# A decoder layer on one Trainium2 core: a second buffer for transposed probabilities, maxima of two heads in one instruction, and another order of the cross-attention loop

## The chip, the core and the metric

The kernel runs on one core of a Trainium2 chip. The metric is the device time of one execution in microseconds (us), the median of several runs. The engines are PE (TensorE, matmuls and transposes), DVE (VectorE), ACT (ScalarE), POOL (GpSimd) and SP (SyncE, which issues most DMAs).

## What is computed

A pre-norm decoder layer over 8 sequences of 100 tokens and width 512, all in float32. The part that matters here is the cross-attention, with 16 heads of size 32 and 345 context tokens:

```python
x = x + self_attention(layernorm(x))            # 16 query heads, 4 key/value heads
q = ln(layernorm(x) @ Wq + bq)                  # per head of 32
k, v = ln(y_main @ Wk + bk), y_main @ Wv + bv   # 345 context tokens, width 256
s = einsum('bhqd,bhkd->bhqk', q, k) * SCALE
p = softmax(s, axis=-1)
ctx = einsum('bhqk,bhkd->bhqd', p, v)           # + the same over 16 further tokens (dca)
x = x + ctx @ Wo + bo
x = x + shared_expert(h) + sum of 4 of 60 routed experts, h = layernorm(x)
```

## The kernel before

The eight sequences are done in four pairs by a hardware loop (`Fori(0, PAIRS)`). Within a pair, PE first does self-attention and the key/value projections of the context, while POOL normalises the heads of the keys and of the queries one after the other (`head_norm` in the POOL program, L654 to L678). Then comes the cross-attention loop, which the change edits. After the last pair follow the router, the shared expert and the routed experts.

The cross-attention loop has ten steps, t = 0 to 9. A "four" is a group of four heads of one sequence; a pair of sequences has eight fours. In step t, PE

- computes the scores of four t (`four_scores`, L913): four products of 32 contraction rows each, into PSUM banks 0 to 3, once ACT has emptied these banks;
- multiplies the values of four t-2 (`four_values`, L935), 12 products, and ahead of four 0 and of four 4 a product of zeros that opens the accumulation in bank 6 or 7 (L930);
- transposes the probabilities of four t-1 (`four_transposes`, L922) in three parts c = 0, 1, 2 of 115 context tokens, alternating between banks 4 and 5;
- runs a hook: in step 0 the query projection of the second sequence (L787), in step 3 the transpose of its normalised queries (L805), in step 4 its scores against the 16 further tokens (L883), in step 5 two more transposes (L891, L947) and the end of the context sum (L900), in step 6 the output projection of the first sequence (L787), in step 8 another transpose (L891).

DVE finds each head's maximum over 345 scores (`four_max`, L1666), ACT computes the exponentials from it (`four_exp`, L1276), and DVE copies the transposed parts from PSUM to SBUF (`four_T`, L1670; part 1 of the last four is copied by ACT, L1325). There is one buffer `xpT` for the three parts. Between these, DVE does pieces of the layer norms of the next pair's inputs (`few(n)` takes n pieces). In step 7 it adds the output projection to the residual (L1637) and starts the last layer norm of the pair. ACT's `q_T(1)` (L1234) copies the second sequence's queries, which the scores of step 4 need.

Each engine runs its own program in the order in which it is written, and semaphores join them. A bank has a "full" and a "free" signal, counted over all fills of the bank in the order that `attention_fills` lists, so the list has to agree with PE's order.

After step 9 the pair ends with a transpose (L781), the router gate and the output projection of the second sequence (together 16 instructions of L787), a residual and a layer norm on DVE, and stores; POOL starts the next pair when the store of x2 has landed (L631).

## Time and profile before

| | us |
|---|---|
| median of 3 runs | 1371.33 |
| lowest and highest | 1367.48, 1371.35 |
| the profiled execution | 1366.12 |
| span in its trace | 1364.3 |

The profile is of one execution. "Granted clock" is the clock that the chip gave TensorE: 1.00 stands for 2.4 GHz and 0.50 for 1.2 GHz. Over the whole span it was 0.88. Matmul ends are modelled, so neighbouring matmul groups overlap slightly in the timeline.

### The profile page before, as it was taken

To read this page: it belongs to the slowest core of one execution; us is meant where nothing else is said; L and a number is where in the kernel's file an instruction comes from. 1 tells how busy PE (TensorE), PEld (TensorE's weight loads), DVE (VectorE), ACT (ScalarE), POOL (GpSimd) and SP (SyncE) were. 2 spreads that over 40 slices of the span, in tenths; PEclk is the share of its full clock that TensorE was granted. 3 is DMA by queue.
4 is the path that set the end of the run, shared out by engine and by line. 5 is a ranking of instruction groups with operands and counts; after the bars stand their busy time and mean duration, and the time that the engine had idled before them with its cause. 6 is when DMAs were issued, how large, how long until landed. Compare 5 with 4: busy or idle time off the path is not lost.

```text
span 1364.3 us, 18670 instructions
## 1 busy us (share of the span) xinstructions
PE 1165.7 (85%) x5358; PEld 617.7 (45%) x5358; DVE 493.3 (36%) x1360; ACT 251.2 (18%) x788; POOL 396.6 (29%) x917
## 2 busy tenths in 40 slices
PE   2988989888899899898879989999898989989920
PEld 0444564446544465444646544335444444444400
DVE  7342645337553474526644601002121212111224
ACT  0141321323231241413312000001010101111100
POOL 4686206852088403874000170000000000000045
PEclk8999679986899877997679998999898989999965
DMA  9997000000100001002027285008999999999835
GB/s 317 341 392 273 1 20 32 22 0 1 33 19 22 0 2 51 1 1 83 1 79 197 70 268 217 0 0 318 386 386 381 387 389 392 387 383 390 323 107 149
DMA packets 76438, 232.71 MB, mean 171 GB/s; under 512 B 11346, under 2 KB 13750, under 8 KB 68670
## 3 DMA queue, kind: packets, MB, share of 16 engines
q1 hardware_dynamic: 58686, 197.55, 40.0%
q10 hardware_dynamic: 11520, 20.98, 4.3%
q0 software_dynamic: 6144, 13.13, 3.3%
q8 instruction: 41, 0.67, 0.2%
q14 instruction: 47, 0.39, 0.1%
HBM read 178.40 MB, written 53.22 MB: 170 GB/s over the span
## 4 chain that ended last, share of the span: by engine, by line
PE 48%; POOL 18%; DMA 11%; issue 11%; DVE 6%; SPq 2%; POOLq 2%; ACT 1%; DVEq 0%; ACTq 0%
PE ps L1048 9%; DMA arena<-in_w 7%; PE ps L1125 6%; PE ps L1098 6%; PE ps L1121 5%; PE ps L787 4%; POOL arena L663 4%; PE ps L922 3%; PE ps L1156 3%; PE ps L1152 3%; DMA arena<-ys_d,slot_u 2%; PE ps L913 2%; POOL arena L660 2%; PE ps L935 2%; POOL arena L685 2%
## 5 line engine op out<-in xcount | busy, mean ns | idle before, releaser
L787 PE MATMUL ps<-arena 128*100 128x512 f32 (+3 forms) x576 | 233.8, 562 | 5.6 <-ACT arena L1223 3.7
L734 POOL DMA_INDIRECT arena<-ys_d,slot_u x32 | 34.6, 1082 | 503.1 <-issue 498.4
L787 PEld LDWEIGHTS ps<-arena 128*100 128x100 f32 (+1 forms) x576 | 95.1, 188 | 121.7 <-issue 111.5
L1125 PE MATMUL ps<-arena 128*64 128x352 f32 x640 | 115.4, 520 | 29.0 <-issue 17.0
L1048 PE MATMUL ps<-arena 128*128 128x400 f32 x352 | 126.4, 519 | 15.2 <-issue 8.3
L869 PE MATMUL ps<-arena 128*100 128x512 f32 x256 | 114.5, 592 | 0.0
L1874 DVE COPY arena<-ps 128x512 f32<-128x512 f32 x40 | 27.7, 692 | 229.0 <-PE ps L1113 229.0
L1048 PEld LDWEIGHTS ps<-arena 128*128 128x128 f32 x352 | 69.2, 198 | 71.0 <-issue 22.0
L1121 PE MATMUL ps<-arena 128*128 128x352 f32 x320 | 98.0, 459 | 1.2 <-DVE arena L1874 1.2
L1125 PEld LDWEIGHTS ps<-arena 128*64 128x64 f32 x640 | 53.5, 154 | 83.2 <-issue 63.4
L1276 ACT ACTIVATE arena<-ps,arena 100x345 f32<-100x345 f32 x128 | 69.1, 546 | 119.2 <-DVE arena L1666 118.7
L922 PE MATMUL ps<-ident,arena 100*115 100x100 f32 x384 | 75.2, 354 | 11.1 <-DVE arena L1670 11.1
L1098 PE MATMUL ps<-arena 128*100 128x512 f32 x176 | 75.8, 592 | 0.7 <-DVE arena L1853 0.7
L1368 ACT ACTIVATE arena<-ps 128x352 f32<-128x352 f32 x40 | 18.6, 465 | 312.9 <-PE ps L1121 168.8
L922 PEld LDWEIGHTS ps<-ident,arena 100*115 100x115 f32 x384 | 64.5, 254 | 24.1 <-DVE arena L1670 12.7
L1121 PEld LDWEIGHTS ps<-arena 128*128 128x128 f32 x320 | 59.2, 190 | 31.0 <-DVE arena L1868 1.4
L869 PEld LDWEIGHTS ps<-arena 128*100 128x100 f32 x256 | 42.0, 167 | 59.7 <-issue 57.3
L1666 DVE TENSOR_REDUCE arena<-ps 100x1 f32<-100x345 f32 x128 | 60.8, 508 | 20.3 <-PE ps L913 19.2
L1670 DVE COPY arena<-ps 115x400 f32<-115x400 f32 x92 | 52.6, 572 | 41.6 <-PE ps L922 41.5
L723 POOL DMA_INDIRECT xs_d<-arena,slot_u x32 | 31.9, 998 | 104.6 <-DVE ov_i L1841 95.1
L663 POOL TENSOR_TENSOR arena<-arena 115x256 f32<-115x256 f32 (+7 forms) x128 | 57.7, 451 | 10.0
L1156 PE MATMUL ps<-arena 128*64 128x512 f32 (+1 forms) x240 | 56.0, 601 | 0.7 <-DVE arena L1890 0.7
(209 smaller groups left out, 1456.6 us busy)
## 6 DMA issues: line engine op xcount, KB each, us to landing
arena<-in_w SPq DMA_DIRECT2D x60, 1408.0 KB, 12.6
arena<-in_w SPq DMA_DIRECT2D x60, 512.0 KB, 13.6
xs_d<-zero SPq DMA_DIRECT2D x5, 3328.0 KB, 26.0
arena<-in_w SPq DMA_DIRECT2D x60, 192.0 KB, 14.3
arena<-xs_d ACTq DMA_DIRECT2D x40, 256.0 KB, 8.0
ys_d<-arena ACTq DMA_DIRECT2D x40, 256.0 KB, 7.6
ys_d<-zero SPq DMA_DIRECT2D x2, 3328.0 KB, 24.8
arena<-in_se_up SPq DMA_DIRECT2D x11, 512.0 KB, 3.4
```

Source lines behind the costliest of these rows:

```text
L663: then(nc.gpsimd.tensor_tensor(s3[:, :, 0:w], s3[:, :, 0:w], s3[:, :, w:2 * w], ALU.add))
L787: last = nc.tensor.matmul(ps[0:m, k, 0:cols[1] - cols[0]], lhs(c), w[:, c, cols[0]:cols[1]], start=(c == 0), stop=(c == n_c - 1))
L869: last = nc.tensor.matmul(ps[0:S, j, :], cT[c % 2][:, g, :], w_out[:, c * G + g, :], start=(c == 0 and g == 0), stop=(c == KV - 1 and g == ...
L922: last = nc.tensor.transpose(ps[0:LC, k, r * S:(r + 1) * S], xp[(4 * t + r) % NP_][0:S, c * LC:(c + 1) * LC], ident[0:S, 0:S])
L1048: last = nc.tensor.matmul(ps[:, (u % 3) * 2 + gu, 0:400].rearrange("p (a b) -> p a b", a=4), se_w[m % 3][:, c, gu * P:(gu + 1) * P], tok, ...
L1098: last = nc.tensor.matmul(ps[0:S, b % 4, :], hT_all[:, m, b * S:(b + 1) * S], w_down[:, m, :], start=(m == 0), stop=(m == MC - 1))
L1121: last = nc.tensor.matmul(ps[:, 1 + gu, 0:I], xsT[0][:, c, :], w13_s[s][0][:, c, at:at + I], start=(c == 0), stop=(c == DC - 1))
L1125: last = nc.tensor.matmul(ps[half * HALF:(half + 1) * HALF, 3 + gu, 0:I], xsT[1][:, c, half * HALF:(half + 1) * HALF], w13_s[s][1 + half][ ...
L1156: last = nc.tensor.matmul(ps[half * HALF:(half + 1) * HALF, 7, :], hT[1][0:w, n, half * HALF:(half + 1) * HALF], w2_s[s][1 + half][0:w, n, :],
L1276: nc.scalar.activation(xp[(4 * t + r) % NP_][0:S, :], ps[0:S, k, 0:LM], ACT.Exp, bias=xnm[0:S, j, h:h + 1], scale=1.0, accum_out=xsum[0:S, ...
L1666: nc.vector.tensor_reduce(xnm[0:S, j, h:h + 1], ps[0:S, k, 0:LM], AX, ALU.max, negate=True).then_inc(xmax_ready.sem, 1)
L1670: nc.vector.tensor_copy(xpT[0:LC, c, :], ps[0:LC, k, 0:4 * S]).then_inc(free[k].sem, 1)
```

## The change

It does five things.

1. `xpT` becomes two buffers, taken in turns by t % 2. The second lies over `kr` and the vector behind it, which the loop does not use.
2. On PE, the transposes of parts 0 and 1 come ahead of the values (and ahead of the product of zeros), and `attention_fills` is reordered to match.
3. Part 1 of every four is copied by ACT, after the four exponentials of the step; DVE copies parts 0 and 2.
4. DVE finds the maxima of two heads in one instruction over two banks, and both instructions stand ahead of the copies; in steps 6 and 7 the multiplication of the context (L1675) and the residual (L1637) stand behind the maxima and ahead of the copies.
5. The product of zeros uses all 128 contraction rows in place of one.

```diff
     for t in range(STEPS):
         if t < FOURS:
             out += [(("xs", t, r), r) for r in range(4)]
+        parts = [(("xpT", t - 1, c), 4 + (t * LN_ + c) % 2) for c in range(LN_)] if 1 <= t <= FOURS else []
+        out += parts[:2]
         if t in (2, 6):
             out.append((("ctx", (t - 2) // 4), 6 + (t - 2) // 4))
-        parts = [(("xpT", t - 1, c), 4 + (t * LN_ + c) % 2) for c in range(LN_)] if 1 <= t <= FOURS else []
-        out += parts[:2] + [(key, 7 if t < 6 else 6) for key in STEP_HOOKS.get(t, [])] + parts[2:]
+        out += [(key, 7 if t < 6 else 6) for key in STEP_HOOKS.get(t, [])] + parts[2:]
...
-        xpT = pT.rearrange("p a b c -> p (a b c)")[:, 0:LN_ * 4 * S].rearrange("p (a b) -> p a b", a=LN_)
+
+        behind_kr = arena[:, kr_at:kr_at + LN_ * 4 * S]
+        assert LN_ * 4 * S <= 3 * D
+        xpT = [v.rearrange("p (a b) -> p a b", a=LN_) for v in (pT.rearrange("p a b c -> p (a b c)")[:, 0:LN_ * 4 * S], behind_kr)]
...
-                        nc.tensor.matmul(ps[:, 6 + j, 0:DC * S], zero[0:1, 0:P], zero[0:1, 0:DC * S], start=True, stop=False)
+                        nc.tensor.matmul(ps[:, 6 + j, 0:DC * S], zero[:, 0:P], zero[:, 0:DC * S], start=True, stop=False)
...
-                    if t >= 2:
-                        four_values(t - 2)
                     if 1 <= t <= FOURS:
                         four_transposes(t - 1, 0)
                         four_transposes(t - 1, 1)
+                    if t >= 2:
+                        four_values(t - 2)
...
+                def four_T(t):
+                    k = filled("xpT", t, 1)
+                    nc.scalar.activation(xpT[t % 2][0:LC, 1, :], ps[0:LC, k, 0:4 * S], ACT.Copy).then_inc(free[k].sem, 1)
+
                 for t in range(FOURS):
...
+                    if t:
+                        four_T(t - 1)
                     if t == 3:
                         q_T(1)
-                k = filled("xpT", FOURS - 1, 1)
-                nc.scalar.activation(xpT[0:LC, 1, :], ps[0:LC, k, 0:4 * S], ACT.Copy).then_inc(free[k].sem, 1)
+                four_T(FOURS - 1)
...
                 def four_max(t, r):
                     j, h = t // 4, 4 * (t % 4) + r
-                    k = filled("xs", t, r)
-                    nc.vector.tensor_reduce(xnm[0:S, j, h:h + 1], ps[0:S, k, 0:LM], AX, ALU.max, negate=True).then_inc(xmax_ready.sem, 1)
+                    for q in range(2):
+                        k = filled("xs", t, r + q)
+                    nc.vector.tensor_reduce(xnm[0:S, j, h:h + 2], ps[0:S, k - 1:k + 1, 0:LM], AX, ALU.max, negate=True).then_inc(xmax_ready.sem, 2)
...
                     four_max(t, 0)
-                    four_max(t, 1)
+                    few(1 if t else 0)
+                    four_max(t, 2)
                     if t == 6:
                         context_T(0)
-                    few(1 if t else 0)
-                    four_max(t, 2)
-                    if t:
-                        four_T(t - 1, 0)
-                    four_max(t, 3)
                     if t == 7:
                         residual("xo", 0)
                         run(pieces)
                         dve.wait_ge(x1_ready, i * 2 + 4)
                         pieces = norm_x(0)
                     if t:
-                        for c in (1, 2):
+                        for c in (0, 2):
                             few(2)
                             four_T(t - 1, c)
```

How the instructions stand, on PE, from the scores of step 3 to the last transposes of that step (L913 scores, L935 values, L922 transposes, L805 the hook; REGISTER_ALU rows prepare waits). Before:

```order
L913 MATMUL ps<-arena 100x345 x4
L935 MATMUL ps<-arena 32x100 x4
L409 REGISTER_ALU
L935 MATMUL ps<-arena 32x100 x4
L409 REGISTER_ALU
L935 MATMUL ps<-arena 32x100 x4
L922 MATMUL ps<-ident,arena 115x100 x8
L765 REGISTER_ALU
L805 MATMUL ps<-ident,arena 128x100 x4
L765 REGISTER_ALU
L922 MATMUL ps<-ident,arena 115x100 x4
```

The same step with the change (L918 scores, L927 transposes, L940 values, L810 the hook):

```order
L918 MATMUL ps<-arena 100x345 x4
L770 REGISTER_ALU
L927 MATMUL ps<-ident,arena 115x100 x4
L770 REGISTER_ALU
L927 MATMUL ps<-ident,arena 115x100 x4
L940 MATMUL ps<-arena 32x100 x12
L770 REGISTER_ALU
L810 MATMUL ps<-ident,arena 128x100 x4
L770 REGISTER_ALU
L927 MATMUL ps<-ident,arena 115x100 x4
```

The values moved behind the first eight transposes, so that they stand between parts 0 and 1 and part 2.

On DVE in step 7, from the second maximum to the first piece of the layer norm (L1666 maxima, L1670 copy, L1637 residual, L1470 first piece). Before:

```order
L1666 TENSOR_REDUCE arena<-ps 100x1
L403 REGISTER_ALU
L1666 TENSOR_REDUCE arena<-ps 100x1
L403 REGISTER_ALU
L1670 COPY arena<-ps 115x400
L1666 TENSOR_REDUCE arena<-ps 100x1
L403 REGISTER_ALU
L1636 REGISTER_ALU
L1637 TENSOR_TENSOR arena<-arena,ps 100x512
L1729 REGISTER_ALU
L1470 BN_STATS arena<-arena 100x6
```

With the change, from the second instruction of maxima to the copy of part 0 (L1677 maxima, L1647 residual, L1480 first piece, L1681 copy):

```order
L1677 TENSOR_REDUCE arena<-ps 100x2
L408 REGISTER_ALU
L1646 REGISTER_ALU
L1647 TENSOR_TENSOR arena<-arena,ps 100x512
L1736 REGISTER_ALU
L1480 BN_STATS arena<-arena 100x6
L1444 REGISTER_ALU
L1483 MEMSET arena 100x1
L1484 BN_AGGR arena<-arena 100x2
L408 REGISTER_ALU
L1681 COPY arena<-ps 115x400
```

The copy of part 0 moved from between two maxima to behind the residual and two pieces of the layer norm.

## Rows read from the trace of the kernel before

**Rows 1.** The page: busy time of each engine, share, instructions.
```profile
PE 1165.7 (85%) x5358; PEld 617.7 (45%) x5358; DVE 493.3 (36%) x1360; ACT 251.2 (18%) x788; POOL 396.6 (29%) x917
```
**Rows 2.** The chain that ended last, pieces in order of time: start, length, what.
```profile
215.43 0.80 POOL arena L636 x3
...
296.42 1.05 POOL arena L677
297.52 0.58 PE ps L805 x4
...
326.35 1.49 PE ps L913 x8
327.83 1.16 PE ps L935 x24
328.99 1.80 PE ps L922 x8
```
**Rows 3.** Windows from the scores of step 2 to those of step 7, four pairs.
```profile
core 0: us, PE busy (x) PEld busy (x) DVE busy (x) ACT busy (x) POOL busy (x), PEclk, DMA share, GB/s
148.55:186.42 37.87, 36.85 (x258) 25.60 (x258) 22.98 (x69) 13.31 (x44) 5.77 (x16) 0.55 0.01 2
313.13:346.30 33.17, 32.12 (x258) 22.21 (x259) 22.71 (x69) 13.31 (x44) 5.78 (x16) 0.65 0.01 2
474.11:506.87 32.76, 30.70 (x258) 20.68 (x258) 22.58 (x69) 13.31 (x44) 5.79 (x16) 0.70 0.01 2
636.71:674.60 37.89, 36.84 (x259) 25.57 (x259) 22.98 (x69) 13.32 (x44) 5.78 (x16) 0.55 0.01 2
```
**Rows 4.** The source line L913: what ended PE's idle time before the scores (us, times).
```profile
  ACT arena L1234: 3.0, 4
  ACT arena L1276: 1.9, 4
```
**Rows 5.** Timeline of PE and DVE in step 1: start, length, instruction, [idle before it, releaser].
```profile
309.45 0.94 DVE L1666 TENSOR_REDUCE arena<-ps 100x1 f32<-100x345 f32 x2
310.31 0.68 DVE L1470 BATCH_NORM_STATS2 arena<-arena 100x6 f32<-100x512 f32 x1
...
311.32 0.57 DVE L1670 COPY arena<-ps 115x400 f32<-115x400 f32 x1
...
311.94 0.65 PE L922 MATMUL ps<-ident,arena 100*115 100x100 f32 x4 [2.21 <-DVE arena L1670]
```
**Rows 6.** Timeline of PE, DVE and ACT in steps 7 and 8.
```profile
349.33 0.65 PE L922 MATMUL ps<-ident,arena 100*115 100x100 f32 x4 [0.56 <-DVE arena L1670]
...
349.62 0.68 DVE L1637 TENSOR_TENSOR arena<-arena,ps 100x512 f32<-100x512 f32 x1
350.42 0.69 DVE L1470 BATCH_NORM_STATS2 arena<-arena 100x6 f32<-100x512 f32 x1
...
351.87 0.38 PE L935 MATMUL ps<-arena 115*32 115x100 f32 x8 [1.59 <-DVE arena L1670]
352.66 0.38 PE L935 MATMUL ps<-arena 115*32 115x100 f32 x8 [0.41 <-DVE arena L1670]
...
354.22 0.51 ACT L1325 ACTIVATE arena<-ps 115x400 f32<-115x400 f32 x1 [3.85 <-PE ps L922]
```
**Rows 7.** Windows of 5 us inside and around the loop, columns as in rows 3.
```profile
155.00:160.00 5.00, 4.99 (x45) 3.72 (x46) 4.86 (x18) 1.94 (x7) 0.00 (x0) 0.50 0.01 2
...
180.00:185.00 5.00, 5.00 (x26) 2.92 (x18) 1.48 (x3) 1.13 (x4) 0.00 (x0) 0.70 0.01 3
185.00:190.00 5.00, 4.44 (x51) 2.85 (x49) 3.35 (x8) 1.84 (x7) 0.00 (x0) 1.00 0.00 0
...
310.00:315.00 5.00, 2.52 (x13) 1.59 (x14) 4.51 (x16) 2.45 (x8) 3.76 (x14) 0.77 0.01 3
```
**Rows 8.** Timeline of PE: products of zeros, and the output projection of step 6.
```profile
314.36 1.53 PE L930 MATMUL ps<-zero 1*128 1x400 f32 x2
...
340.08 0.83 PE L930 MATMUL ps<-zero 1*128 1x400 f32 x2
...
342.38 3.60 PE L787 MATMUL ps<-arena 128*100 128x512 f32 x8
...
181.97 4.13 PE L787 MATMUL ps<-arena 128*100 128x512 f32 x8
```
**Rows 9.** Costliest groups of the page: busy us, mean ns, idle before.
```profile
L1666 DVE TENSOR_REDUCE arena<-ps 100x1 f32<-100x345 f32 x128 | 60.8, 508 | 20.3 <-PE ps L913 19.2
L1670 DVE COPY arena<-ps 115x400 f32<-115x400 f32 x92 | 52.6, 572 | 41.6 <-PE ps L922 41.5
```
**Rows 10.** The chain that ended last: gate and output projection at the end of pairs 0 and 2.
```profile
201.02 4.37 PE ps L787 x16
...
521.19 7.61 PE ps L787 x16
```

More of the change, by code:

```diff
@@ L197, in decoder_kernel @@
         qr = [carve(D) for _ in range(2)]
+        kr_at = top[0]
         kr = [carve(KV, G, HD) for _ in range(2)]
@@ L935, in four_values @@
                             nc.tensor.matmul(ps[r * HD:(r + 1) * HD, 6 + j, a * S:(a + 1) * S], vx[j][0:LC, c, h * HD:(h + 1) * HD],
-                                             xpT[0:LC, c, r * S:(r + 1) * S], start=False, stop=False)
+                                             xpT[t % 2][0:LC, c, r * S:(r + 1) * S], start=False, stop=False)
                 def context_end(j):
@@ L1664, in four_max @@
                     j, h = t // 4, 4 * (t % 4) + r
-                    k = filled("xs", t, r)
-                    nc.vector.tensor_reduce(xnm[0:S, j, h:h + 1], ps[0:S, k, 0:LM], AX, ALU.max, negate=True).then_inc(xmax_ready.sem, 1)
+                    for q in range(2):
+                        k = filled("xs", t, r + q)
+                    nc.vector.tensor_reduce(xnm[0:S, j, h:h + 2], ps[0:S, k - 1:k + 1, 0:LM], AX, ALU.max, negate=True).then_inc(xmax_ready.sem, 2)
                 def four_T(t, c):
                     k = filled("xpT", t, c)
-                    nc.vector.tensor_copy(xpT[0:LC, c, :], ps[0:LC, k, 0:4 * S]).then_inc(free[k].sem, 1)
+                    nc.vector.tensor_copy(xpT[t % 2][0:LC, c, :], ps[0:LC, k, 0:4 * S]).then_inc(free[k].sem, 1)
                 def context_T(j):
```

## Prediction

> **What bounds the kernel now.** I read the page first. PE is busy 85% of the span and DVE 36% [rows 1], but that is a mean over stages with different limits. So next I read the chain of waits in order of time, for one pair. From 215.43 to 297.47 us it consists mostly of POOL instructions: the head norms, which the change does not touch. From 297.52 on it goes through PE: query transpose, scores, values, transposes [rows 2]. The loop ends in a layer norm and a store, and POOL starts the next pair only after that store. So a microsecond saved in the loop is saved once in each of the four pairs and is not made up for elsewhere; after the last pair the router follows, which waits for the same things.
>
> Inside the loop I compared the four pairs over the same work, from the scores of step 2 to the scores of step 7 [rows 3]. The work is the same and the time is not: 37.87, 33.17, 32.76 and 37.89 us. The column of the granted clock goes with it: 0.55, 0.65, 0.70, 0.55. PE is busy 36.85 of 37.87 us in the first pair. Here the reader is to see that the loop is bound by PE at the lower level of its clock, and that waits are a small part: 1.02 us in pair 0 and 2.06 us in pair 2. Where PE waits for copies, the waits stand at three places: before the last transposes of step 1 [rows 5], before the scores of steps 2 and 4 [rows 4], and around steps 7 and 8 [rows 6].
>
> 0.3% of this kernel, about 4.1 us, is what a measurement can tell from no change.
>
> **The maxima.** 128 instructions of 508 ns [rows 9] become 64. Two in a row now take 0.94 us from start to end [rows 5]. An instruction over 690 scores does not occur. 345 elements take 0.508 us and the 512 of the layer norm's first piece 0.68 us [rows 5, 9], about 1.0 ns an element, so 690 take about 0.86 us. Bounds are 0.69 us (the 512-element piece) and 1.02 us (two whole instructions). DVE saves 0.1 us for two heads. The first exponential of a step starts some 0.4 us later, but the exponentials of a step are needed one step later, so ACT hides it. I cost this at nothing.
>
> **The copies.** 28 copies of 572 ns [rows 9] leave DVE and become ACT copies of 0.51 us [rows 6]. ACT is busy 13.3 of 33 to 38 us in the loop [rows 3], and DVE 23. The ACT copy stands behind four exponentials, and behind it stand the exponentials of the next step, whose scores come later anyway. In step 3 `q_T(1)` is queued behind it too, but this also waits for a PE transpose that stands behind the values. I cost the copies at nothing; if PE came to run at the higher level throughout, each could cost its 0.51 us in the steps that ACT then bounds. The second buffer adds no wait.
>
> **The wait of step 4.** The scores of step 4 wait for `q_T(1)`, 3.0 us over four pairs [rows 4]. It comes late because the fourth exponential of step 3 waits for the fourth maximum, which is queued behind a copy that waits for transposes behind the values. With all maxima ahead of the copies, ACT is free when the transpose arrives. I take -3.0 us (bounds 0 and -3.0).
>
> **Step 1 gets a little worse.** Now the copy of part 0 starts at 311.32, behind three maxima and one piece of layer norm, and the last transposes wait 2.21 us for it [rows 5]. With the change two instructions of 0.86 us, the piece and two further pieces (0.35 us together) stand ahead: 309.45 + 0.86 + 0.6 + 0.86 + 0.35 is 312.1, 0.8 us later. The scores of step 2, which wait now for the fourth exponential (1.9 us over four pairs [rows 4]), then wait for nothing but PE. Net I take +0.3 us a pair, +1.3 us in all (bounds 0 and +3.2).
>
> **Steps 7 and 8.** Now PE waits 0.56 us, then 1.59 and 0.41 us [rows 6], 2.56 us a pair. With the change both instructions of maxima, the residual (0.7 us) and two pieces (0.9 us) stand ahead of the copy of part 0. Counted from the scores of step 7 at 346.30 [rows 3]: 0.85 for the scores, 1.7 for the maxima, 0.2 for a wait in between, 0.7, 0.9 and the copy's 0.57 make 351.2. Now the copy has ended when PE goes on at 349.33 [rows 6], so the last transposes of step 7 wait some 2.4 us. But the transposes of step 8 now come ahead of the values, so the 1.59 and 0.41 us go, and the last values start some 0.5 us earlier. I take -0.5 us a pair, -2.0 us in all (bounds -6 and +3.2). The order alone thus gives -3.0 + 1.3 - 2.0 = -3.7 us.
>
> **The product of zeros and the clock.** The product costs what it did: its two instructions take 0.83 us at the higher level over 400 columns; eight full-height ones over 512 columns take 3.60 us there [rows 8], 0.45 each, which for 400 columns is 0.35, or 0.70 for two. Height is free. What it does to the clock is the main term. In pair 0 the clock is 0.50 through the loop's steps 2 to 6, although PE has hardly a gap; it rises during the output projection of step 6, a run of full-height products [rows 7, 8], and falls in stretches in which PE waits, as in the last of the windows [rows 7]. What stands between in the loop are products with 32 rows or 32 columns, transposes, and a product of one row [rows 8]. The change puts a full-height product of 1.53 us (at the lower level [rows 8]) into step 2 and into step 6. I expect that the clock rises soon after step 2 in each pair and again in step 6, as it did by luck in pairs 1 and 2. The price comes from rows 3: pairs 0 and 3 take 37.9 us at 0.55, pairs 1 and 2 take 33.2 us at 0.65 and 32.8 us at 0.70. If pairs 0 and 3 come to 33.2, that is 2 x 4.7 = 9.4 us; I cost pairs 1 and 2 at nothing, since from 0.65 to 0.70 the time hardly falls: DVE with 23 us of work and its waits becomes the bound. I take -9.4 us. Bounds: 0 if the clock takes no notice; -9.4 and 3 us more in each pair, -21.4 us, if no pair stays at the lower level for over a step or two.
>
> The Trainium skill's page "TensorE: Matmul & The Clock Gate" (Part 1, "What's actually happening") says that the gate is set by how busy PE has been recently. Read as it stands, it speaks against this term: height would change nothing, and the sum would be the order's alone. The trace doesn't agree with that reading: PE was busy 4.99 of 5.00 us at a clock of 0.50 [rows 7].
>
> **The sum.** -3.7 - 9.4 = -13.1 us. The profiled execution took 1366.1 us, so its like would take 1353.0. It lies 5.2 us under the median of 1371.3 and 1.4 us under the lowest of the three runs. Which pairs have luck with the clock may differ from run to run, so I start from the mean of the three, 1370.1, and get **1357.0 us**.
>
> **The rivals.**
>
> - *The clock takes no notice* of the height of a product whose factors are zeros; only the order counts: 1370.1 - 3.7 = 1366.4 us. For it: the loop was bound by PE with gaps of only 1 to 2 us in 33 to 38 [rows 3], so order alone can give little. Against it: only runs of full-height products went ahead of the rise in pair 0. This is also the case that follows from the page's rule as cited. Chance 0.22.
> - *Slower: the copies come too late.* Every copy of part 0 is now behind both maxima and up to two and a half microseconds of residual and norm. If PE's wait ahead of the last transposes of step 7 exceeds the 2.56 us that it replaces, and the clock falls in it, then pair ends run at the lower level: gate and projection take 7.61 us there against 4.37 [rows 10], +3.2 us in pair 0, +1.6 in pair 1, +0.5 in pair 3. With +1.3 in step 1, +3.2 in steps 7 and 8 and -3.0 in step 4 that makes +6.8: 1376.9 us. For it: the wait of 2.21 us in step 1 is followed by a fall of the clock [rows 5, 7]. Against it: the clock falls in step 8 as it is, so there is little left to lose. Chance 0.12.
> - *DVE becomes the bound.* If the clock is high everywhere, the loop is limited by DVE and the time per pair stays near 29 to 30 us: the low end, 1345 us. This is part of my forecast's case.
>
> **How the numbers follow.** My forecast's case has chance 0.66: from -5 to -25 us, likeliest -13. The page-like case, 0.22, lies around -4, between -9 and +1, and is split between faster and the same. The slow case has 0.12. The range reaches from 1345 (-25) to 1369 (the top of the second case); outside lie the slow case and little more. Faster by over 0.3%: 0.63 + 0.10 = 0.73. Within 0.3%: 0.03 + 0.12 + 0.02 = 0.17. Slower: 0.10.
>
> **What would show it.** In the profile after, over the stretch from the scores of step 2 to those of step 7, all four pairs should take 30 to 33.5 us at a granted clock of 0.65 or more, the clock should be up within a step of the product of zeros, the wait for `q_T(1)` should be gone, and one maximum over two banks should take 0.8 to 0.9 us. In step 7 PE should wait over 2 us ahead of the last transposes. The prediction is wrong if pairs still stand at 0.55 and 38 us (the first rival), if the ends of pairs get longer by over a microsecond (the second), or if POOL's part of a pair changes in length.

## The result and the profile after

The change is slower: 1380.6 us median (1372.0 to 1387.1, 12 runs) against 1363.1 us (1350.3 to 1371.7, 12 runs) of before on the same chip, ratio 1.0145 with an interval of [1.0115, 1.0175], some 17 to 20 us. The lowest of the 12 runs of the change (1372.04) lies above the highest of before (1371.71). Forecast were 1357.0 us, between 1345 and 1369, and "faster". The profiled execution took 1380.59 us with a span of 1378.8; that of before 1366.12 with 1364.3. (Runs of one kernel spread by up to 3% on some chips, and the ratios leave disturbed runs out; where a ratio rests on few runs, the ratio of the medians of all runs stands beside it below, as "medians".)

The page after, busy time of each engine (of before: [rows 1]):

```profile
PE 1159.5 (84%) x5358; PEld 611.7 (44%) x5358; DVE 480.0 (35%) x1268; ACT 259.4 (19%) x816; POOL 397.5 (29%) x917
```

The windows from the scores of step 2 to those of step 7, the same four stretches as [rows 3], with the change:

```profile
core 0: us, PE busy (x) PEld busy (x) DVE busy (x) ACT busy (x) POOL busy (x), PEclk, DMA share, GB/s
144.60:182.08 37.48, 33.77 (x260) 22.49 (x259) 20.87 (x51) 14.83 (x49) 5.27 (x14) 0.66 0.01 2
309.87:347.79 37.92, 34.39 (x260) 22.75 (x259) 20.80 (x51) 14.99 (x50) 5.64 (x16) 0.64 0.00 0
477.07:513.23 36.16, 32.85 (x259) 22.07 (x259) 19.91 (x51) 14.98 (x50) 5.64 (x16) 0.67 0.01 2
644.47:682.34 37.87, 34.42 (x260) 22.78 (x259) 20.72 (x51) 14.98 (x50) 5.64 (x16) 0.64 0.01 2
```

Pairs 0 and 3 got the clock they lacked (0.55 before, 0.66 and 0.64 now) and are no shorter; pairs 1 and 2 had 0.65 and 0.70 already and are 4.7 and 3.4 us longer. PE's idle time (length less PE busy) is 3.3 to 3.7 us where it was 1.0 to 2.1. Over the four pairs this stretch takes 149.4 us, where before it took 141.7. The second pair step by step, windows of steps 2 to 6:

```profile
309.87:315.17 5.30, 5.30 (x48) 3.30 (x47) 4.65 (x11) 2.78 (x10) 4.28 (x15) 0.68 0.00 0
315.17:322.05 6.88, 3.78 (x49) 2.62 (x49) 5.80 (x18) 3.20 (x10) 0.58 (x1) 0.88 0.00 1
322.05:328.79 6.74, 6.74 (x52) 5.10 (x52) 2.70 (x8) 2.62 (x9) 0.00 (x0) 0.50 0.00 0
328.79:337.53 8.74, 8.31 (x59) 6.37 (x58) 5.03 (x11) 3.46 (x11) 0.79 (x1) 0.50 0.00 0
337.53:347.79 10.26, 10.26 (x56) 5.36 (x55) 2.62 (x4) 2.93 (x10) 0.00 (x0) 0.67 0.00 0
```

This is the table to learn from. In step 3 the clock is at its higher level for most of the step (0.88) and PE has only 3.78 us to do, yet the step takes 6.88 us: DVE is busy 5.80 of it, and PE waits 3.1. The clock is at 0.50 again before the step ends and stays there for steps 4, 5 and part of 6. Here a clock that rose while another engine set the pace bought nothing, and it did not stay.

Where PE waits, from the timeline of PE, steps 1, 3, 4 and 7 of the same pair:

```profile
309.30 0.65 PE L927 MATMUL ps<-ident,arena 100*115 100x100 f32 x4 [2.99 <-DVE arena L1681]
...
320.11 0.82 PE L927 MATMUL ps<-ident,arena 100*115 100x100 f32 x4 [1.97 <-DVE arena L1681]
...
322.05 1.49 PE L918 MATMUL ps<-arena 32*100 32x345 f32 x8 [1.13 <-ACT arena L1239]
...
352.90 1.05 PE L927 MATMUL ps<-ident,arena 100*115 100x100 f32 x8 [2.65 <-DVE arena L1681]
...
354.22 0.80 PE L927 MATMUL ps<-ident,arena 100*115 100x100 f32 x4 [0.27 <-DVE arena L1681]
```

Against the same pair before ([rows 5, 6], 0.54 us at the scores of step 2, 0.53 at those of step 4): step 1 +0.78, step 2 -0.54, step 3 +1.97, step 4 +0.60, steps 7 and 8 +0.36 (2.56 before, 2.92 now), together +3.2 us in this pair. The groups of the page (of before: [rows 9]):

```profile
L927 PE MATMUL ps<-ident,arena 100*115 100x100 f32 x384 | 74.6, 351 | 30.6 <-DVE arena L1681 30.6
...
L1677 DVE TENSOR_REDUCE arena<-ps 100x2 f32<-100x690 f32 x64 | 54.1, 868 | 30.0 <-PE ps L918 27.7
...
L1681 DVE COPY arena<-ps 115x400 f32<-115x400 f32 x64 | 36.6, 572 | 56.8 <-PE ps L927 56.8
```

PE sits idle 30.6 us behind DVE's copies; before it was 11.1 us at the transposes (L922) and 8.0 at the values (L935), 19.1 together. An instruction of maxima takes 868 ns.

**An account for all runs.** I cut each profiled execution into loops (first scores of a pair to its last residual), gaps (from there to the next pair's first scores), and the rest. The kernels named here are those of the experiments below; "again" is a second profile of the same kernel. For loops and gaps I summed PE's idle time and the time at the lower clock (1.2 GHz). A window over the first loop of the change shows how:

```profile
132.84:200.82 67.98, 57.94 (x436) 37.63 (x437) 36.77 (x96) 25.17 (x82) 10.33 (x26) 0.72 0.03 10
```

Idle time is 67.98 - 57.94 = 10.0 us; a mean clock of 0.72 means the lower level for 2 x (1 - 0.72) of it, 38 us (37.4 by the clock's own records, which the table uses). One line for each execution, four loops and three gaps, in us:

```
                   loops   gaps    sum   PE idle  low clock  sum - idle - low/2
before             273.3   287.3  560.6   53.8     186.9       413
before_again       268.2   287.4  555.6   52.7     178.5       414
the change         275.4   293.2  568.6   64.3     180.7       414
after_again        276.5   293.2  569.7   64.9     178.4       416
z_only             279.2   286.6  565.8   57.5     191.0       413
no_z               291.3   293.7  585.0   53.4     238.3       412
copies_first       268.0   291.1  559.1   60.4     164.6       416
cf_again           270.6   292.5  563.1   59.1     175.3       416
cf_old_pe          265.3   291.3  556.6   60.6     158.3       417
cf_no_z            286.4   288.7  575.1   46.7     231.2       413
max_only           274.3   289.8  564.1   51.5     204.4       410
act_copy           282.4   290.1  572.5   53.1     216.3       411
copies_first_7     286.4   286.6  573.0   62.9     189.5       415
copies_first_1to6  272.4   289.6  562.0   58.7     174.1       416
before_z_every     264.6   290.2  554.8   57.4     112.6       441
after_z_every      258.4   288.5  546.9   64.3      86.2       440
cfo_z_every        249.0   288.7  537.7   59.7      66.8       445
cfo_z_every_again  256.9   294.5  551.4   58.8     101.5       442
```

The last column hardly moves (410 to 417; 440 to 445 with 24 more products). It is PE's work counted at the higher clock, so the account is bookkeeping: it says where the time is, and not why. Two quantities carry nearly all of the difference between these kernels: PE's idle time, and half of the time at the lower clock. The change has as much low clock as before (180.7 and 178.4 against 186.9 and 178.5) and 11 us more idle time. Within that, the loops have on the mean of the two profiles 17 us less low clock, and the gaps 14 more.

The idle time has its place too. In the loops it is 40.2 us in both profiles of the change and 29.0 in both of before. Of these 11.2 us, in the first pair of profiles, 8.8 stand between the scores of step 2 and those of step 7 (14.0 us over four pairs, against 5.2), 3.1 in step 1 and 0.9 in steps 7 and 8, while 1.5 went away at the scores of step 2.

In the first pair of profiles loops and gaps differ by 8.0 us and the routed rounds, which the change does not touch, by 8.1 (369.2 before, 377.3 after); everything else is 1.6 us shorter, which makes the 14.5.

### The profile page after: what moved, and what is told of

Same layout as the page of the kernel before. It is cut to its first block, busy times and chain, and to the rows that moved or that the text cites. A ratio compares the mean times of both kernels' runs of the same rounds, so it can differ in the third digit from the quotient of the medians.

```text
span 1378.8 us, 18670 instructions
## 1 busy us (share of the span) xinstructions
PE 1159.5 (84%) x5358; PEld 611.7 (44%) x5358; DVE 480.0 (35%) x1268; ACT 259.4 (19%) x816; POOL 397.5 (29%) x917
## 3 DMA queue, kind: packets, MB, share of 16 engines
q1 hardware_dynamic: 58686, 197.55, 40.2%
## 4 chain that ended last, share of the span: by engine, by line
PE 45%; POOL 18%; DMA 14%; issue 11%; DVE 6%; SPq 3%; POOLq 2%; ACT 1%; DVEq 0%; ACTq 0%
DMA arena<-in_w 9%; PE ps L1053 9%; PE ps L1103 5%; PE ps L1130 5%; PE ps L1126 4%; PE ps L792 4%; POOL arena L668 4%; PE ps L927 3%; DMA arena<-ys_d,slot_u 3%; PE ps L1161 3%; PE ps L1157 2%; POOL arena L665 2%; PE ps L918 2%; POOL arena L690 2%; PE ps L940 2%
## 5 line engine op out<-in xcount | busy, mean ns | idle before, releaser
L927 PE MATMUL ps<-ident,arena 100*115 100x100 f32 x384 | 74.6, 351 | 30.6 <-DVE arena L1681 30.6
L927 PEld LDWEIGHTS ps<-ident,arena 100*115 100x115 f32 x384 | 63.6, 251 | 57.9 <-DVE arena L1681 33.4
L1677 DVE TENSOR_REDUCE arena<-ps 100x2 f32<-100x690 f32 x64 | 54.1, 868 | 30.0 <-PE ps L918 27.7
L1681 DVE COPY arena<-ps 115x400 f32<-115x400 f32 x64 | 36.6, 572 | 56.8 <-PE ps L927 56.8
```

The costliest lines, as they stand in the source:

```text
L927: last = nc.tensor.transpose(ps[0:LC, k, r * S:(r + 1) * S], xp[(4 * t + r) % NP_][0:S, c * LC:(c + 1) * LC], ident[0:S, 0:S])
L1677: nc.vector.tensor_reduce(xnm[0:S, j, h:h + 2], ps[0:S, k - 1:k + 1, 0:LM], AX, ALU.max, negate=True).then_inc(xmax_ready.sem, 2)
L1681: nc.vector.tensor_copy(xpT[t % 2][0:LC, c, :], ps[0:LC, k, 0:4 * S]).then_inc(free[k].sem, 1)
```

## The experiments

**The kernel before again.** No edit.

> The kernel before once more, as a second profile of the same program. It tells what part of the 14.5 us between the two spans belongs to the change. If the loss is in the cross-attention loop and its pair, the stretch from the first scores of pair 0 to those of pair 3 takes 485 to 490 us here, as before (488.2), against 498.9 with the change, and the routed experts differ between executions by some microseconds either way. If the loss is outside the loop (the routed experts took 8 us longer in the profile with the change), this profile has the routed experts at 358 us as before and never near 366. Ratio to before 1.00, within 0.3%.

1345.9 us against 1346.9, 0.9962 [0.9916, 1.0008]. A kernel against itself can so come out 0.4% off. And the loop is not repeatable: pair 0 took 33.18 us from step 2 to step 7 where it took 37.87 in [rows 3], and pair 1 took 35.8 where it took 33.2; pairs 2 and 3 took the same again. The luck with the clock belongs to the execution at least as much as to the pair. From the first scores of pair 0 to those of pair 3 it took 483.2 us, even less than the 485 expected, where the change took 498.9 and, in after_again, 500.0. Its routed rounds took 367 us, 2 less than in the first profile.

**The zero product alone, and all but the zero product.**

```
z_only = before with, no_z = the change without:
-  nc.tensor.matmul(..., zero[0:1, 0:P], zero[0:1, 0:DC * S], start=True, stop=False)
+  nc.tensor.matmul(..., zero[:, 0:P], zero[:, 0:DC * S], start=True, stop=False)
```

> The kernel before with the full-height product of zeros alone. Theory 1, late copies (the DVE order costs what is lost, the product of zeros gains): pairs 0 and 3 come down from 38 us to some 33 to 34 us over steps 2 to 7, total 5 to 15 us faster than before. Theory 2, the clock (raising the clock early in the loop is itself what hurts, since it ends in a stretch in which PE waits and is granted the lower level for longer): total the same or up to 8 us slower.

> The changed kernel with the product of zeros back to one row. Theory 1: slower than before by more than the change is, 1.5 to 2.5%, with the waits for the copies of part 0 as in the change but with pairs at 0.55 and 38 to 40 us. Theory 2: as fast as before or a little faster, within 0.5%.

z_only 1.0065 [1.0033, 1.0098], as its theory 2 had it; no_z 1.0187 [1.0126, 1.0249], as its theory 1 had it in time; of the change's waits for copies it has those of steps 1 and 7 (2.99 and 2.65 us) and not that of step 3. The order is what costs, and the product gives part of it back: loops and gaps take 585.0 us without it and 569 with it (in time the intervals of no_z and of the change, on other chips, overlap). Alone the product costs too. The windows from step 2 to step 7 of no_z, pairs 0 and 1:

```profile
149.94:190.21 40.27, 39.43 (x259) 25.73 (x259) 20.78 (x51) 14.98 (x50) 5.58 (x16) 0.53 0.01 2
322.01:363.36 41.35, 40.51 (x260) 26.14 (x259) 20.86 (x51) 14.84 (x49) 5.29 (x14) 0.52 0.01 1
```

PE waits here only 0.8 us. The new order without the product has no more idle time than before (28.9 us in the loops, 29.0 before), but never gets the rise of the clock in step 5 that before has in its good pairs: low time in the loops 213.9 us against 167 to 177. This is no luck of one execution: the mean granted clock of the four runs of no_z is 0.873 to 0.877, that of the 25 runs of before on the same chip 0.886 to 0.903. In z_only the product raised the clock in pairs 1 and 3 and did nothing in pairs 0 and 2. Its pairs 0 and 1 from step 2 to step 7:

```profile
146.74:182.94 36.20, 35.18 (x262) 23.89 (x262) 22.66 (x69) 13.29 (x44) 5.71 (x16) 0.59 0.01 2
312.58:349.02 36.44, 32.66 (x258) 21.29 (x258) 22.94 (x69) 13.30 (x44) 5.76 (x16) 0.67 0.01 2
```

PE idles 3.8 us where the clock rose and 1.0 where it did not, and the pair is no shorter. That is with DVE's order of before, and it is as much as in any pair of the change. Steps 2, 3 and 4 of pair 1:

```profile
312.58:318.96 6.38, 5.57 (x47) 3.03 (x47) 4.23 (x15) 2.34 (x8) 4.97 (x15) 0.73 0.00 0
318.96:325.48 6.52, 3.98 (x49) 2.83 (x49) 6.31 (x23) 2.91 (x9) 0.00 (x0) 0.82 0.01 4
325.48:331.96 6.48, 6.48 (x52) 5.02 (x53) 3.44 (x12) 2.34 (x8) 0.00 (x0) 0.50 0.01 3
```

The same picture as after: at the higher clock DVE, 6.31 of 6.52 us busy, sets step 3; the clock falls. PE waits 1.50 us there for a copy that stands where it always stood, and 1.04 us for `q_T(1)`:

```profile
323.34 1.10 PE L922 MATMUL ps<-ident,arena 100*115 100x100 f32 x4 [1.50 <-DVE arena L1670]
...
325.48 1.49 PE L913 MATMUL ps<-arena 32*100 32x345 f32 x8 [1.04 <-ACT arena L1234]
```

**Copies ahead of the pieces.** The change with DVE's order of a step rewritten; twice, the second time beside the change on one chip.

```
 four_max(t, 0)
-few(1 if t else 0)
 four_max(t, 2)
+if t: four_T(t - 1, 0)
 if t == 6: context_T(0)
+few(3 if t else 0)
+if t: four_T(t - 1, 2)
 if t == 7: residual, run(pieces), wait, norm_x(0)
-if t: for c in (0, 2): few(2); four_T(t - 1, c)
+           (in step 7 also few(2))
 few(2 if t else 0)
```

> The changed kernel with DVE's copy of part 0 straight behind the two instructions of maxima, fewer pieces of layer norm between the copies, and the residual and first pieces of the pair's last layer norm behind both copies. Theory 1: PE's waits for the copy of part 0 fall from 2.99 to some 1.7 us in step 1 and from 2.65 to under 1 us in step 7, PE's idle time before the transposes from 30.6 us to 15 us or less, total 10 to 18 us faster than the changed kernel. Theory 2: the waits fall but the total stays within 4 us of the changed kernel's.

> The kernel copies_first once more, on the chip of after_again. Theory 1: 0.997 to 1.003 of before and 1.0 to 1.8% below the change. Rival (chip and execution): level with the change.

> The change once more, beside copies_first on one chip. Theory 1 (late copies): the change is at 1.012 to 1.018 of before again, and 1.010 to 1.018 above copies_first. Rival (the chip and the execution, not the order): the change comes out within 0.5% of copies_first, and the 1.45% was a matter of the chip it was measured on. In the profile: of the 14.5 us by which the profiled execution of the change was longer than that of before, 8.1 lay in the routed rounds, whose instructions the change does not touch and where the memory queues are busy throughout (385 GB/s before, 374 after in the same 100 us); if that part is an accident it comes back to 367 to 369 us here, if it hangs on the change it stays at 375 to 378.

copies_first 1.0000 [0.9971, 1.0029], cf_again 1.0027 [0.9979, 1.0075], the change again 1.0111 [1.0005, 1.0216] over four runs (medians: 0.9998 and 1.0066; 1350.4 us against 1359.5). The change is slower on this chip too, by less, and the new order of DVE's step gives it back: 0.7% by the medians, between the 1.0 to 1.8% of the theory and the 0.5% of the rival, and some 8 us of loops and gaps. PE in pair 1 of cf_again, steps 1, 3, 4 and 7:

```profile
311.52 0.65 PE L927 MATMUL ps<-ident,arena 100*115 100x100 f32 x4 [2.07 <-DVE arena L1681]
...
321.35 0.65 PE L927 MATMUL ps<-ident,arena 100*115 100x100 f32 x4 [0.48 <-DVE arena L1681]
...
323.69 1.49 PE L918 MATMUL ps<-arena 32*100 32x345 f32 x8 [1.69 <-ACT arena L1239]
...
351.02 0.65 PE L927 MATMUL ps<-ident,arena 100*115 100x100 f32 x4 [1.01 <-DVE arena L1681]
```

At the copies 2.99, 1.97 and 2.65 us have become 2.07, 0.48 and 1.01, and over the launch PE waits for DVE's copies 13.9 us in place of 30.6, as forecast. But its idle time in loops and gaps falls only from 64.3 and 64.9 to 60.4 and 59.1. Most of the waits moved: the scores of step 4 wait 1.7 us for `q_T(1)` in every pair, those of step 2 wait 0.44 again, and in step 7 0.75 us for ACT's copy and up to 1.22 at the next hook come in. So early copies give back 5 of the 11 us of idle time; the rest of the gain is low clock (164.6 and 175.3 us in place of 180.7 and 178.4, half of which counts). Nor is the order of the copies all that the edit changes. It also moves the pieces of layer norm, and with them go seven or eight DVE instructions slowed beside POOL in each profile of the change (last section). What part of step 3's gain is theirs, no run separates.

The routed rounds of after_again took 364.9 us, less than the 369.2 of before, so nothing ties the 8.1 us there to the change. Its gaps stood at 293.2 again, 6 us above before.

**Which step's copies.** The edit above in step 7 alone, and in steps 1 to 6 alone.

> The change with DVE's copies ahead of pieces and residual in step 7 alone; steps 1 to 6 as in the change. In the profile of the change PE idles 2.65 us behind DVE's copy in step 7, 2.99 in step 1, 1.97 in step 3 (pair 1), against 0.56 and 2.21 and nothing before. Theory 1a, the late copy of step 7 is the larger part (residual, pieces and norm stand ahead of it there): this kernel gains 1.5 us or more a pair of loop length on the change, 6 us a launch, 0.4 to 0.6% below it. Theory 1b, the earlier steps are the larger part (the copies behind both maxima and a piece in six steps): under 0.3% below the change.

> The mirror of copies_first_7: copies first in steps 1 to 6, step 7 as in the change. Theory 1a: under 0.3% below the change, with the 2.65 us of step 7 still there. Theory 1b: 0.4 to 0.7% below the change, with the waits of step 1 and 3 at 2.1 and 0.5 us as in cf_again, and the 2.65 us still there.

1.0163 [1.0063, 1.0263] and 1.0111 [1.0042, 1.0180] (medians 1.0086 and 1.0052). The change itself did not run on this chip, and four runs each don't separate the two. There is only the account of one profile each: loops and gaps 573.0 and 562.0 us against 568.6 and 569.7 of the change, idle time 62.9 and 58.7 against 64.3 and 64.9. By the idle time steps 1 to 6 are the part that pays. The low clock is a weaker witness: in pair 2 of copies_first_7 the clock did not rise at the product of step 2, with the same instructions in steps 1 to 6 as in the change, and stayed low for 34 us. In copies_first_7 the waits of step 7 are down as in cf_again, but then PE waits 0.75 us for ACT's copy and 1.22 for DVE at the next hook, so nothing is won; the steps before have 2.99 and 1.57 still. In copies_first_1to6:

```profile
310.40 0.65 PE L927 MATMUL ps<-ident,arena 100*115 100x100 f32 x4 [2.07 <-DVE arena L1681]
...
320.26 0.65 PE L927 MATMUL ps<-ident,arena 100*115 100x100 f32 x4 [0.51 <-DVE arena L1681]
...
351.56 1.05 PE L927 MATMUL ps<-ident,arena 100*115 100x100 f32 x8 [2.65 <-DVE arena L1681]
```

(Its routed rounds took 379.3 us, those of copies_first_7 362.3 on the same chip: that part varies by itself.)

**TensorE's order, and the product of zeros once the copies are early.** cf_old_pe is copies_first with `four_values(t - 2)` ahead of the transposes again, in the fills too; cf_no_z is copies_first with the one-row product.

> The kernel copies_first (1.000 of before), with TensorE's order of before: the values of step t-2 stand ahead of the transposes of step t-1 again, and the fills with them. Theory 1, the order on TensorE has a price of its own: in the profile of the change steps 4 and 5 took 6.74 and 8.74 us where before they took 6.48 and 8.55, without a wait among them, so some 0.25 us a step, 6 steps, 4 pairs = 6 us; then this kernel is at 0.995 to 0.997 of before, and steps 4 and 5 at the lower clock come back to about 6.5 and 8.55 us. Rival, the order is worth its place: with the values ahead, the transposes come later, the copies behind them too, and the projection of the next values waits longer; then this kernel is at 1.003 to 1.008. If neither, 1.000.

> The kernel copies_first with the zero product of one row again. Theory 1: in the order of the change the full-height zero product helped by 0.4% (the change at 1.0145, without it 1.0187 of before on another chip), since the lower clock else holds for 37 to 40 us of steps 2 to 7 of each pair; then this kernel is at 1.004 to 1.008 of before, and the clock does not rise in step 2 of any pair. Rival, the zero product hurts wherever TensorE does not wait otherwise (z_only stood at 1.0065): then this kernel is at 0.993 to 0.997.

On this chip, here and for the single parts below, before's 13 runs spread from 1336.5 to 1376.5 us and the ratios rest on four of them; the medians are the safer numbers. cf_old_pe 1.0096 [1.0036, 1.0156], but medians 1361.3 and 1361.1 us: in time undecided, and the gain of 0.3 to 0.5% that was expected is not there. In the profile steps 4 and 5 at the lower clock are 6.48 (pair 2) and 8.55 us (pairs 0 and 3) as expected, where copies_first has 6.73 and 8.74 without a wait among step 4's: that is 0.2 us a step at that clock for the new order, read in one profile. The Trainium skill's page "TensorEngine Tiling (Array Packing)" says that a change of tiling mode drains TensorE, and the new order puts another kind of product between values and hook; no run here tells that cause from others. cf_no_z 1.0267 [1.0100, 1.0434] (medians 1.014): more than I expected; the clock rose in step 2 of no pair, and first 41 to 50 us after the first scores. Its four runs, at a mean granted clock of 0.869 to 0.872 where before's lowest is 0.881, are as long as before's longest or longer. With the new order the product is needed.

**Single parts on the kernel before.** max_only has the maxima of two heads in one instruction and nothing else; act_copy has the second buffer and ACT's copy of part 1 in each step, and nothing else.

> The kernel before with only the maxima of two heads in one instruction, everything else in its old place; the order on DVE becomes maxima of heads 0 and 1, one piece, maxima of 2 and 3, copy of part 0, pieces and copies. 64 instructions of 0.86 us in place of 128. Theory 1: the maxima themselves cost nothing, and the copy of part 0 is where it was: 0.998 to 1.002 of before, PE idle in steps 2 to 7 at 1 to 2 us a pair as before. Rival, the pairing itself is the loss: ACT cannot start on head 0 before head 1 has its maximum and the copy of part 0 stands behind all four, so the same 10 us or so go as in the change: 1.006 to 1.010, and PE idle of 3 us or more a pair behind DVE's copies.

> The kernel before with only the second buffer of transposed probabilities and the copy of part 1 on ACT in every step (28 more copies a launch on ACT, 28 fewer on DVE); DVE, TensorE and the maxima as before. Theory 1: in the change the 3.0 + 1.9 us of waits for q_T(1) and the exponential became 4.8 for q_T(1) alone, so ACT's copy ahead of q_T(1) gives away about what it wins elsewhere: 0.998 to 1.003 of before. Rival, ACT's copies are what makes the change slow: 1.006 or more, with PE waiting for ACT. Rival, DVE is relieved and TensorE waits less: 0.993 to 0.997.

1.0159 [0.9945, 1.0373] and 1.0215 [1.0042, 1.0389] (medians 1.0063 and 1.0110). max_only is inconclusive in time; in the profile PE idles 27.5 us in the loops against 29.0, so the pairing adds no wait, which rules the rival's mechanism out. act_copy is slower, and neither as the theory nor as the rival had it: PE's idle time is 30.2 us in the loops against 29.0, while low clock is 195.5 against 167 to 177. In pair 0 the rise came 49.0 us after the first scores, in before's at 47.0 and in before_again's at 35.2, so one pair says little. The runs say more: their mean granted clock is 0.874 to 0.880, below each of the 13 runs of before on this chip (0.881 to 0.908). That of max_only is 0.880 to 0.898. So ACT's copies, with the second buffer, are enough to lower the clock. Which part of the order does so in no_z, and whether TensorE's order has a share, no run separates.

**The zero product in every step.** If height sets the clock and one product holds it for a stretch only, several should hold it.

```
 if a == 0:
     begin("ctx", j)
-    nc.tensor.matmul(..., zero[:, 0:P], zero[:, 0:DC * S], start=True, stop=False)
+nc.tensor.matmul(..., zero[:, 0:P], zero[:, 0:DC * S], start=(a == 0), stop=False)
```

> cf_old_pe (copies first, TensorE's order of before) with a full-height zero product ahead of the values in every step and not only in fours 0 and 4 (6 more a pair, each 0.53 us at the higher clock and 0.89 at the lower). In the profiles so far the length of the loop of steps is 39 to 40 us + PE's idle time + half of the time at the lower clock, to within 0.7 us in nearly every pair. Theory 1, the clock is what sets the loop, and height sets the clock: the lower clock in steps 2 to 7 falls from 17 to 23 us a pair to under 10, worth 5 us or more, against 3 us of added products of which the idle time takes some: 1 to 4 us a pair, 0.992 to 0.998 of before. Rival, another engine takes over as soon as the clock is up: PE idle in steps 2 to 7 grows from 4 to 7 us or more, and nothing is won: 1.000 to 1.008. Rival, a zero product in every step does not hold the clock up: it falls after 7 us as before, and the kernel is 12 us or more longer: 1.009 or more.

> The kernel before with a full-height zero product in every step, nothing else. Theory 1 (the clock sets the loop and height sets the clock): low time in steps 2 to 7 falls from 20 to 34 us a pair to under 12, worth 8 us or so, against 3 us of products: 0.990 to 0.997. Rival, the engines beside it take over, DVE first (it carries four maxima of 0.5 us, three copies of 0.5 us and the pieces in each step): PE idle of 6 us or more in steps 2 to 7, 1.000 to 1.008. Rival, it does not hold the clock up: 1.010 or more, as z_only (1.0065) and worse.

> The change, DVE's order and all, with a full-height zero product in every step. Loops and gaps of the change sum to 568.6 and 569.7 us in two profiles, of before to 560.6 and 555.6; PE's idle time in them is 64.3 and 64.9 against 53.8 and 52.7, its time at the lower clock 180.7 and 178.4 against 186.9 and 178.5. Theory (late copies cost 11 us of idle time, the clock is a lever apart from them): the low time falls by 80 us or more, the idle time stays at 65 or above, the sum comes to 545 to 558 and the kernel to 0.993 to 1.003 of before: it gets back what the copies lose, and stays 0.5 to 1% above cfo_z_every. Rival (with the clock up, DVE is the bound, and its late copies cost more): 1.005 or more.

> cfo_z_every once more, in five rounds on another chip, as a version that may beat both kernels: 0.988 to 0.996 of before if the 0.9929 was no accident of its chip; rival, 0.998 or more.

On cf_old_pe 0.9929 [0.9880, 0.9979], and on another chip 0.9974 [0.9933, 1.0014] (medians 0.9898 and 0.9921), the second between what was hoped for (0.996 or less) and its rival (0.998 or more). On before 0.9987 [0.9944, 1.0030] (medians 0.9949), not clear of before: low clock from step 2 to 7 was 16 us in three of its pairs where under 12 was expected. On the change 0.9990 [0.9940, 1.0041] (medians 0.9959). The windows from step 2 to step 7 of cfo_z_every:

```profile
145.92:176.85 30.93, 26.82 (x265) 16.34 (x265) 20.81 (x54) 15.07 (x50) 5.94 (x17) 0.94 0.01 2
303.48:335.80 32.32, 29.67 (x265) 18.04 (x265) 20.28 (x54) 15.13 (x50) 5.96 (x17) 0.85 0.01 2
463.56:494.50 30.94, 26.80 (x265) 16.32 (x265) 20.83 (x54) 15.08 (x50) 5.96 (x17) 0.94 0.01 2
619.94:654.03 34.09, 29.92 (x264) 18.60 (x264) 20.86 (x54) 15.16 (x50) 5.96 (x17) 0.85 0.01 2
```

30.9 to 34.1 us against 36.2 to 37.9 of the change, at a granted clock of 0.85 to 0.94. Low clock in this stretch is 3.4 to 10.2 us a pair, in seven of the eight pairs of the two executions; in the eighth it is 26.5, and that pair takes 39.3 us. That is close to the theory's forecast. With the change's own late copies low clock falls by 92 us (86.2 from 178.4) and the idle time stays at 64.3, also as forecast; but the kernel comes within 0.2% of cfo_z_every on the same chip (0.4% by the medians), where 0.5 to 1% was expected. cfo_z_every is the fastest version here. It beats the change, and on one of two chips it beats before by more than the interval.

The expectation put a product at 0.53 us. That is one instruction, and a product is two: 0.94 us at the higher clock, 1.70 at the lower, where the product of one row took 0.83 and 1.53 [rows 8]. The first line is from cfo_z_every, the second from z_only.

```profile
328.43 0.94 PE L934 MATMUL ps<-zero 128*128 128x400 f32 x2
313.72 1.70 PE L930 MATMUL ps<-zero 128*128 128x400 f32 x2
```

## Why the prediction was wrong

- **The maxima, 0 us.** Right: 868 ns measured, 0.86 us estimated, and in max_only PE waits no longer than before.
- **Step 1 and the scores of step 2.** "Net I take +0.3 us a pair": +0.78 - 0.54 = +0.24. Right.
- **Steps 7 and 8, -0.5 us a pair.** The wait ahead of the last transposes of step 7 was forecast at 2.4 us and is 2.65; the 1.59 and 0.41 us at the values went as forecast. But in pair 1 another 0.27 came, and 2.56 became 2.92: +0.4. The mechanism was right, the term of the wrong sign by its size. copies_first_7 shows how little hangs on it.
- **The wait of step 4, -3.0 us.** Failed. "With all maxima ahead of the copies, ACT is free when the transpose arrives", yet the wait for `q_T(1)` is 4.8 us, where `q_T(1)` and the exponential together took 4.9 [rows 4]. It hangs on the clock: 1.7 us over four pairs in no_z, where the clock stays down, and in z_only 1.04 us in a pair whose clock rises in step 2 against 0.49 in one where it does not. With the clock up in step 3 the scores want to start earlier, and `q_T(1)` does not come earlier with them.
- **The copies, "I cost the copies at nothing".** Failed. I looked for who waits for ACT's copies and priced DVE's only where the trace of before had a wait, in steps 1 and 7. In step 3 nothing waited before, since PE ran at the lower clock and DVE had time. With the clock up, PE waits 1.97 us there. That belonged to the same sum as the clock: the sentence "DVE with 23 us of work and its waits becomes the bound" was applied to pairs 1 and 2 only. How much of it is the late place of the copies? z_only has them in their old place and waits 1.50 us in the same step, and earlier copies give back 5 of the 11 us of idle time. The larger part is the clock that rises into DVE's pace.
- **The product and the clock, -9.4 us.** This is the step on which the forecast fails: the stretch that was to give 9.4 us takes 7.7 us more. Half of the mechanism held. The clock rises within 4 us of the start of the product of step 2 in all eight pairs of the two profiles of the change and in none of no_z, and a product in every step holds it up. What failed is "If pairs 0 and 3 come to 33.2": pairs 1 and 2 had their 33 us from a rise in step 5, when PE has work at the higher clock (in pair 2 the clock was up in step 3 as well, for 3.4 us). A rise ahead of step 3 meets DVE's bound and falls again after some 7 us, and the later one then comes at 44 to 47 us after the first scores instead of 34 to 35. Low clock from step 2 to 7 fell only from 111.2 to 104.2 us over four pairs, worth 3.5 us, against 8.8 us more idle time in the same stretch, and the gaps gained 15.5 us of low clock, worth 7.8.
- **"The product costs what it did", "Height is free".** Nearly: 1.70 us against 1.53 at the lower clock, 0.94 against 0.83 at the higher, about 1 us over the eight products.
- **"The order alone thus gives -3.7 us."** Failed: no_z stands at 1.0187. Its idle time is that of before, so no wait that I could have summed shows it; with the new order the clock stays low until after the loop. The lucky rise of before was taken as given, and it hung on the order of the instructions. Why is open; act_copy, with its lower clock, points at ACT's copies as one part of it.
- **The rivals.** "The clock takes no notice" is refuted. "The copies come too late" named one part of the cause at a price of 6.8 us, where the idle time grew by 11, and put it into steps 7 and 8, where it is least. Its chance of 0.12 was too low: it and the clock term were treated as separate cases, although a clock that rises is what makes the copies late. For the rule of the Trainium skill's page "TensorE: Matmul & The Clock Gate" that was cited against the term, the runs bear out the trace: PE is busy 39.43 of 40.27 us in no_z at 0.53.

What stays open is the size: 1.0145 on one chip, 1.0111 on another (medians 1.0128 and 1.0066), while loops and gaps differ by 8 to 14 us, 0.6 to 1.0%. The gaps are 6 us longer by low clock alone: 24 us of it in both profiles against 11 before, worth 7, with the same idle time to within 2 us. Most of it lies 38 to 53 us behind the loop's end; why the clock falls there is open. In the profile of the change PE also idles 0.9 and 1.5 us with no releaser where the loop over pairs turns, in two of three turns. In after_again it does not, and in some other kernels it does once, so this is not the change's:

```profile
367.66 0.90 PE L786 MATMUL ps<-ident,arena 100*128 100x100 f32 x8 [0.88 <-issue]
```

## What to carry to other kernels

Where an engine runs at two clocks, price the change twice, once at each: look at what the other engines need per step (here DVE 5.8 us) before you count a faster PE as gain. Here each rise that ended in such a wait was lost within 7 us. A run of good luck in the profile is a result of the present order, not a floor to start from: take the same stretch over several pairs and executions. And put the copy that the slowest engine waits for ahead of everything that nobody waits for, but add up the idle time of the whole stretch afterwards: here 17 us of waits went at the copies, and 12 came back at other places.

## What the runs showed of the hardware

- Height counts for the clock here, and busy time alone does not raise it: no_z is at 0.53 with PE busy 98% of the stretch. The product of step 2 with 128 rows was followed by a rise within 4 us in 23 of 24 pairs with TensorE's new order (the change, copies_first and its parts) and in four of eight with the old one (z_only, cf_old_pe); with one row, in none of 24 pairs of six profiles. So the order around it seems to count too. A product of zeros in every step took the low time in loops and gaps from 158 us (cf_old_pe) to 67 and 102. Of the 28 us by which the last column of the account grew, the 24 products are some 22 (0.94 us each at the higher clock).
- Small DVE instructions are slow beside wide ones of POOL. From the timeline of the change, steps 2 and 3 of pair 1:

```profile
313.65 1.04 POOL L682 TENSOR_TENSOR arena<-arena 100x512 f32<-100x512 f32 x1
313.70 1.02 DVE L1468 TENSOR_TENSOR arena<-arena 100x1 f32<-100x1 f32 x1
...
314.66 1.09 POOL L697 TENSOR_TENSOR arena<-arena 100x512 f32<-100x512 f32 x1
314.75 1.01 DVE L1471 TENSOR_TENSOR arena<-arena 100x1 f32<-100x1 f32 x1
```

  The same instructions on one column take 0.16 us where POOL works on small ones. They end with POOL's. In this pair they put 1.7 us on DVE's work just ahead of the maxima of step 3; how much later the copies come by it was not measured. The Trainium skill's "GPSIMD Engine Reference" (1. Specifications) says that POOL shares its SBUF interface with VectorE and that instructions with two SBUF inputs contend; the trace agrees for these two. It happened seven or eight times in each profile of the change and of no_z (7 to 8 us a launch) and in copies_first_7 (6 us), and never in before, copies_first and copies_first_1to6, where the pieces stand elsewhere in the step: moving small work can cost when its new place lies beside another engine's wide work.
- The routed rounds, where the memory queues are busy throughout, took 362 to 379 us for the same instructions, 385 GB/s from 1000 to 1100 us of before and 374 in the same window of the change. Such a part has to be taken out before two single profiles are compared.
